# A two-layer transformer forward on one core: each sample's expert routing moved into the attention loop of the next sample

## The reference

```python
h = _layernorm(x) * (1 + ca) + sa
x = x + ga * path_attention(h)          # layer 0, attention: 16 heads of 8
#   L = I + tril(w w^T * beta, -1);  A = solve(L, tril(w k^T, -1))
#   S = q k^T - (q w^T) (beta * A);  P = softmax(S * scale + G_i - G_j, causal);  o = P v
h = _layernorm(x) * (1 + cb) + sb
# layer 0, feed-forward: 16 experts, each token goes to 4
logits = -sum((h - keys) ** 2) + h @ rw.T + rb
topv, topi = top_k(logits, 4);  w = softmax(topv)
x = x + gb * sum(w * (gelu(h @ w1[topi] + b1) @ w2[topi] + b2))
```

## Time and profile before

| | us |
|---|---|
| median of 3 runs (range) | 2480.23 (2475.24 to 2481.59) |
| profiled execution | 2472.11 |
| its span | 2470.3 |
| PE busy | 2084.1 (84%) |
| DVE busy | 1657.9 (67%) |
| POOL busy | 888.7 (36%) |
| ACT busy | 868.9 (35%) |

### The profile page before, as it was taken

The page is one execution under the profiler, slowest core; times in us unless marked ns, Lnnn a source line. Parts: engine busy times, 40 slices in busy tenths (PEclk is TensorE's granted clock), DMA queues, the critical chain, the costliest instruction groups (busy, mean ns, idle before and its releaser), DMA issues. The chain is left out here.

```text
span 2470.3 us, 44381 instructions
## 1 busy us (share of the span) xinstructions
PE 2084.1 (84%) x16530; PEld 1398.4 (57%) x16530; DVE 1657.9 (67%) x3582; ACT 868.9 (35%) x1690; POOL 888.7 (36%) x904
## 2 busy tenths in 40 slices
PE   3888988988988998988988879778799995787885
PEld 2564564654654654644645656545799994344443
DVE  5969579579478488488487444422466665699986
ACT  2031331331331241331332221221165652777782
POOL 1514314225125225125125143632366655433321
PEclk7998988988988988988989887666899997898997
DMA  3105005014023031050050010100622222100000
GB/s 102 35 4 85 2 11 78 2 26 63 2 39 50 3 61 27 3 79 9 3 87 1 16 32 16 34 25 19 219 71 73 72 71 78 49 18 26 5 9 13
DMA packets 133721, 99.85 MB, mean 40 GB/s; under 512 B 13265, under 2 KB 124434, under 8 KB 133394
## 3 DMA queue, kind: packets, MB, share of 16 engines
q1 hardware_dynamic: 124818, 79.05, 16.0%
q0 software_dynamic: 8704, 17.97, 2.2%
HBM read 36.60 MB, written 56.25 MB: 38 GB/s over the span
## 5 line engine op out<-in xcount | busy, mean ns | idle before, releaser
L605 ACT ACTIVATE a_prep<-ps 128x1536 f32<-128x1536 f32 (+1 forms) x112 | 155.7, 1390 | 403.0 <-PE ps L1218 269.6
L832 DVE TENSOR_REDUCE a_mpart<-ps 128x4 f32<-128x512 f32 x320 | 198.7, 682 | 73.4 <-PE ps L1159 46.8
L1761 ACT ACTIVATE b_hid<-ps,b_stage 128x128 f32<-128x128 f32 x576 | 164.0, 368 | 143.2 <-PE ps L1856 130.5
L412 POOL TENSOR_TENSOR a_K<-a_K,a_yU 128x480 f32<-128x480 f32 (+14 forms) x120 | 83.7, 698 | 359.3 <-DVE a_yU L781 358.4
L1746 POOL DMA_INDIRECT rows_y<-b_orow,b_target x144 | 167.0, 1160 | 118.6 <-DVE b_orow L1833 115.2
L418 POOL TENSOR_TENSOR a_X<-a_X,a_flow 128x480 f32<-128x480 f32 (+14 forms) x240 | 181.5, 772 | 77.4 <-DVE a_flow L786 76.4
L1037 PE MATMUL ps<-a_flow,cst 128*128 128x480 f32 (+14 forms) x480 | 180.3, 481 | 6.9 <-DVE a_flow L768 6.1
L1444 POOL DMA_INDIRECT rows_h<-a_flow,r_slot x112 | 108.9, 972 | 177.8 <-DVE a_flow L1612 123.0
L1865 PE MATMUL ps<-b_stage,b_hid 128*128 128x128 f32 x1152 | 153.2, 276 | 1.3 <-ACT b_hid L1761 1.3
L1856 PE MATMUL ps<-b_hTp,b_stage 128*128 128x128 f32 x1152 | 153.9, 277 | 0.0
L1865 PEld LDWEIGHTS ps<-b_stage,b_hid 128*128 128x128 f32 x1152 | 141.0, 193 | 1.7 <-ACT b_hid L1761 1.7
(11 more groups left out here) (466 smaller groups left out, 4641.3 us busy)
## 6 DMA issues: line engine op xcount, KB each, us to landing
rows_h<-a_blank SPq DMA_DIRECT2D x66, 520.0 KB, 12.9
b_hrow<-rows_h SPq DMA_DIRECT2D x144, 65.0 KB
b_w<-in_wexp SPq DMA_DIRECT2D x16, 514.0 KB
c_got<-rows_y SPq DMA_DIRECT2D x32, 256.0 KB, 4.0
rows_y<-b_orow,b_target POOLq DMA_INDIRECT x144
out<-xs SPq DMA_DIRECT2D x8, 256.0 KB, 2.3
cst<-in_const SPq DMA_DIRECT2D x1, 1865.5 KB, 14.7
rows_h<-a_flow,r_slot POOLq DMA_INDIRECT x112
```

Of the source, the lines that this page charges most:

```text
L605: nc.scalar.activation(Pt[:, at:at + width, :], ps[:, 4:4 + width, :], ACT.Exp).then_inc(e_exp.sem, width)
L832: nc.vector.tensor_reduce(mpart[:, i, j, 4 * g:4 * g + 4], ps[:, 4 + n % 4, :].rearrange("p (r j) -> p r j", r=4), AX.X, ALU.max).then_inc ...
L1761: last = nc.scalar.activation(hid[:, p % 2, f, :], ps[:, p % 2, 128 * f:128 * f + 128], ACT.Gelu, bias=stage[:, p % 3, AT_B1 + f:AT_B1 + f ...
```

## The change

The routing of sample b - 1 now runs inside iteration b of the attention loop.

- Iteration 0 is taken out of the loop and has orders of its own for PE and DVE (`ORDER_BEGIN`), with the few steps that begin the routing (`route_begin_vector`, `route_begin_tensor`). The loop is `Fori(1, B - 1)`, six iterations, with `ORDER_ROUTE`, in which r stands beside b and f: 6 letters on PE, 27 on DVE, 8 on ACT and 16 on POOL (its 16 scatters). Taken without r, b and f have the sequence of before.
- In the end stage only sample 6 is routed; its scatters wait one by one for row maxima (`pace`). Sample 7 is routed in the experts, as before.
- The routing's buffers now lie in `mats`, which is free between the 7 chunk steps of the back and the building of the next matrices; `htok` takes its tail. So the norm of the routing waits for the back's chunk steps (`rolled`), the new matrices wait for the routing's end (`V.into`), and those in the tail, 5 of 14, for the landing of the sample's scatters (`R.sent`). Its constants (table 204 KB, b2 8 KB, a gate row 64 KB) are loaded again in each iteration, last in SP's queue.
- The routing's matmuls write PSUM banks 0 to 2, which the front's recurrence uses. So each group of them waits for a step of the recurrence (`gaps`), and six matmuls of the recurrence wait for a routing step (`held`). DVE copies the counts out of PSUM first, and adds into `xs` in 4 pieces.
- `hrows` isn't zeroed in full any more. A region has 640 rows more (EDGE), and after the last slot of sample 6 is given, SP writes 640 rows behind each expert's last row, at an offset read from `R.edge`, and the spare rows: 20 DMAs in the end stage, `R.filled` in the place of `R.zeroed`. `dest` is loaded once, in the first front.

```diff
+ORDER_ROUTE = {
+    'pe': ('bbbbbbbbbfbbbbfbfbfbbbfffbbbbbbbbbbfbbbbbfffbbbbbbbbffbbbfbbbfbbbbfffbbbbbbffbbbbbffbbbbbrbbbbbfbbbb'
...
+    'po': ('bbbbbbbfffffffffffffffbfffbfbbbfbbfrbbrfffrfrffrfffrrfffrfffrrfffrffrffrffrfffrr'),
+}
 ORDER_END = {
...
-    'po': ('bbbbbbbrrrrrrrrrrrrrrrrrrrrrrrrrrrrrrrrrrrrrrrrrrbrrrrrrrrrbbrbbbrbbrbrrrrrrrrrrrrrrrrrrrrrrrrrrrrrr'
-           'rrrrrrrrrrrrrrrrrrrrrrrrrrrrr'),
+    'po': ('bbbbrbbbrrrrrrrrrrbrrrrbrbrbbbbbb'),
 }
...
+        TAIL = 14 * T - NT * TOPK * ROW
+        before_tail = pieces(mats[:, 0:TAIL])
+        table, b2, gate = before_tail(ROUTE["rb"].stop), before_tail(D), before_tail(D)
+        blank = txy[:, 0:EDGE // 128 * ROW]
+        R.place(before_tail(ROUTE_FLAT), table, b2[0:E, :], gate, pieces(mats[:, TAIL:])(NT, TOPK, ROW))
...
-            with sp.Fori(0, B - 1) as b:
-                sp.sem_inc(go.sem, 1)
-                sp.dma_start(gate_row[:, :], dram["s_gate0"][:, bass.ds(b, 1), :]).then_inc(e_gate.sem, 16)
+            gates(0)
+            front()
+            constants(0)
+            close()
+            with sp.Fori(1, B - 1) as b:
+                gates(bass.ds(b, 1))
                 front()
-                for n in range(SHARE):
-                    sp.dma_start(whole[bass.ds(b * SHARE + n, 1)].rearrange("n p f d -> p (n f) d"), blank[:, :].unsqueeze(1).broadcast_to([128, 8, ROW]))\
-                        .then_inc(R.zeroed.sem, 16)
+                constants(bass.ds(b - 1, 1))
                 close()
...
+            gates(B - 1)
+            constants(B - 2)
+            sp.wait_ge(*e_blank())
+            sp.wait_ge(*e_edge())
+            for e in range(E):
+                at = sp.value_load(R.edge[0:1, e:e + 1], min_val=0, max_val=E * CAP - EDGE)
+                sp.dma_start(hrows[bass.ds(at, EDGE), :].rearrange("(p f) d -> p (f d)", p=128), blank).then_inc(R.filled.sem, 16)
...
+            both(2, ORDER)
+            with po.Fori(1, B - 1) as b:
+                both(b + 2, ORDER_ROUTE, b, r=route_pool(nc, po, R, V, hrows))
...
-            weave(ORDER_END['po'], b=back(), r=each(lambda b: route_pool(nc, po, R, hrows, b), B - 1))
+            weave(ORDER_END['po'], b=back(), r=itertools.chain(blanks(), route_pool(nc, po, R, V, hrows, pace=[e_max(8 + 2 * n) for n in range(16)])))
...
                     if over_back and j == 0:
                         ve.wait_ge(*e_kx())
+                    if over_back and j == 0:
+                        ve.wait_ge(*(V.begun() if routing is None else V.into()))
+                    if routing is not None and T * (j + 1) > TAIL:
+                        ve.wait_ge(*R.sent(routing))
...
+                held = {("U", 4): V.hT(), ("X", 5, 0): V.htok(0), ("X", 6, 1): V.logc(), ("U", 7): V.counted(),
+                        ("X", 8, 0): V.turned(), ("X", 9, 1): V.part()} if routing else {("U", 4): V.begun()}
...
+            gaps = {"xT": e_yU(2), "back": e_yX(6), "log": e_yX(9), "count": e_yU(5), "turn": e_yX(12), "bias": e_yX(15)}
+            both(2, ORDER_BEGIN, False, itertools.chain(wait_for(pe, gaps["xT"]), route_begin_tensor(nc, pe, ps, R, V)))
+            with pe.Fori(1, B - 1) as b:
+                both(b + 2, ORDER_ROUTE, True, route_tensor(nc, pe, ps, cst, R, V, gaps))
...
-CAP = B * T
+EDGE = T + PAGE
+CAP = B * T + EDGE
```

More of the change, by code:

```diff
@@ L454, in _, with both @@
             po.sem_inc(over.sem, 1)
-            with po.Fori(0, B - 1) as b:
-                po.wait_ge(go.sem, b + 2)
+            def both(go_at, order, sample=None, **routing):
+                po.wait_ge(go.sem, go_at)
                 po.sem_inc(started.sem, 1)
-                weave(ORDER['po'], b=back(), f=front(True))
+                weave(order['po'], b=back(), f=front(True), **routing)
                 po.wait_ge(*e_uU())
@@ L963, in _, with front @@
             mm = nc.tensor.matmul
-            def front(over_back):
+            def front(over_back, routing=False):
                 pe.wait_ge(*e_xn())
@@ L1278, in _, with both @@
             pe.sem_inc(over.sem, 1)
-            with pe.Fori(0, B - 1) as b:
-                pe.wait_ge(go.sem, b + 2)
+            def both(go_at, order, routing, r):
+                pe.wait_ge(go.sem, go_at)
                 pe.sem_inc(started.sem, 1)
-                weave(ORDER['pe'], b=back(), f=front(True))
+                weave(order['pe'], b=back(), f=front(True, routing), r=r)
                 pe.wait_ge(*e_m())
@@ L1384, in __init__ @@
-        self.e_dest, self.e_share4, self.e_turn, self.e_turned, self.e_bias = ev("dest"), ev("share4"), ev("turn"), ev("turned"), ev("bias")
-        self.e_part, self.e_in = ev("part"), ev("in")
-        self.e_sent = ev("sent", 16 * NT * TOPK)
-    def place(self, table, b2, gate, xn, hT, hsq, part, htok, small, wide, turned):
-        self.table, self.b2, self.gate = table, b2, gate
-        self.xn, self.hT, self.hsq, self.part, self.htok, self.turned = xn, hT, hsq, part, htok, turned
-        take, at = pieces(small), pieces(wide)
+        self.edge = sb("edge", [1, E], I32)
@@ L1484, in route_vector @@
-def route_vector(nc, ve, xs, ps, R, b):
+    act.wait_ge(*V.htok(0))
+    nc.scalar.copy(R.htok[:, :, 1:TOPK, 0:D], R.htok[:, :, 0:1, 0:D].broadcast_to([128, NT, TOPK - 1, D])).then_inc(V.htok.sem, 1)
+    yield
+    act.wait_ge(*V.shift())
+    nc.scalar.activation(R.raw, R.shifted, ACT.Exp).then_inc(V.exp.sem, 1)
+    yield
+    act.wait_ge(*V.turn())
+    nc.scalar.copy(R.turned, ps[0:E, 1, :]).then_inc(V.turned.sem, 1)
+def route_vector(nc, ve, xs, ps, R, V, tile, free=()):
     def line(ap):
@@ L1628, in route_tensor, with gap @@
+    yield
+    ve.wait_ge(*V.part())
+    ve.wait_ge(*V.xn())
+    for t in range(NT):
+        xb = xs[:, tile(t), :]
+        last = nc.vector.tensor_tensor(xb, xb, R.part[:, t:t + 1, :], ALU.add)
+    last.then_inc(V.into.sem, 1)
+def route_tensor(nc, pe, ps, cst, R, V, gaps=None):
     mm = nc.tensor.matmul
     ident = cst[:, CONST["ident"][0]:CONST["ident"][1]]
-    pe.wait_ge(*R.e_xn(b))
-    if b == B - 1:
-        pe.wait_ge(*R.loaded(1))
-    if b:
-        pe.wait_ge(*R.e_hT(b - 1))
+    def gap(name):
+        if gaps:
+            pe.wait_ge(*gaps[name])
+    pe.wait_ge(*V.xn())
+    gap("xT")
@@ L1740, in _ @@
         def _(po):
[L1741 removed]
+            for _ in route_pool(nc, po, R, V, hrows, filled=True):
                 pass
```

555 lines of the change are left out of this document (284 added, 271 removed).

## The result

| | before | after |
|---|---|---|
| median of 4 runs (range), us | 2477.73 (2472.88 to 2481.59) | 2447.10 (2435.78 to 2464.25) |
| ratio (95% interval) | | 0.9881 (0.9846 to 0.9916) |
| profiled execution / span, us | 2472.11 / 2470.3 | 2449.33 / 2447.5 |

The kernel became 1.2% faster, 31 us by the medians, where 100 were forecast; 2447 lies outside the range (2322 to 2440). The direction was right. The runs after spread over 28 us, those before over 9, and the profiled execution after, 2449, lies near their middle.

A forecast was written before the change was run, and what follows sets the result against it. PE was seen as busiest in the loop (161 of 179 us), seven samples' routing as stretching the end stage. End stage -174, loop +78, iteration 0 +1, experts -5 gave -100: 2372, carried to 2378 us; range 2322 to 2440.

The forecast's parts named there:

- The loop: Six attention iterations, each now holding one sample's routing: +13 us an iteration, +78 in all.
- the scatters' term: POOL in the loop: 16 scatters, 20 us, mostly covered by its stalls waiting for DVE; +1 us an iteration.
- The other two terms: Routing's cost in the loop on DVE, +10 us an iteration, and on PE, +2.
- rival 2: Each loop scatter costs the front a share of itself, 8 us an iteration: +48, 2426 us; chance 12%.
- The first leg: In the loop DVE and POOL shut each other out at the shared port: 8 us an iteration.
- The second leg: PE's instructions wait for issue beside scatters: 0.8 us a scatter, 8 us an iteration.
- Rival 4: Loop scatters lie in the front's chain in full, delaying updates, DVE and PE: 33 us an iteration, 2498 us; chance 7%.
- The end stage: Stage after the loop, keeping one sample's routing of seven: from 331 to 157 us, -174.
- the maxima: 40 row maxima of the end stage: 27 us of DVE plus 10.5 of routing, 38 us.
- The other four parts: End stage: start to first maximum 36 us, last maximum to first exp 19, exps 48, last exp to end 16.
- Instruction fetch: Code grows, but queue traffic in the iterations and PEld's wait at the loop's start stay as before: 0.
- The experts: Experts stage: DVE no longer waits 6.02 us for r_dest, -5 us.

The follow-up runs named there:

- e3: Changed kernel without the scatters of samples 0 to 5, only its loop to be read: exps of iterations 2 to 6 52.8 to 54.5 us, six iterations 1155.4 us.
- e8: Changed kernel with two memsets in place of each loop scatter, only its loop to be read: exps of iterations 2 to 6 55.2 to 60.2 us.
- e7: Changed kernel with all 16 scatters of a sample in one burst in the loop, ahead of the updates: ratio 1.0195 against the kernel before.
- e11: Changed kernel with loop written out, scatters later in the exps and no end-stage fillers: 2394.0 us, ratio 0.9916 against the kernel before on its chip.
- e12: Changed kernel with scatters later in the exps and no end-stage fillers, loop kept: 2397.0 us, ratio 0.9924 against the kernel before on its chip.
- e1: Changed kernel with the 20 fills of hrows waiting for the end stage's last row maximum: 2446.2 us, ratio 0.9835 against the kernel before.
- groups 1 and 2: Two sets of four edited versions of the changed kernel, each set on one chip; the kernel before has medians of 2484.8 and 2480.5 us there.
- e5: Changed kernel without the 175 filler matmul steps in TensorE's end stage: 2438.4 us, ratio 0.9739 against the kernel before.

## Why the prediction was wrong

The forecast was -100 and the profiles give -22.8. The 77 us between them are 46 of the loop, 23 of the end stage, 8 of what follows it, less 1 of the first stages.

**The loop (+78, measured +124.3): the step that failed is the scatters' term, +1 an iteration, on the ground that POOL's stalls cover them.** The exps grew by 5.5 to 7.9 us in five iterations and by 19.6 in one, 8.5 on the mean. Without scatters (e3) it is 1.9, with memsets in their place (e8) 4.7, both on other chips' profiles; and the loop without scatters costs +81.7, near the 72 of the forecast without that term. The stall total of the earlier trace rows was no cover: DVE does wait for POOL (19.2 us once with the burst of e7; in the exps of iteration 2 by 2.5 us with the scatters spaced, 0.5 without), PE then waits for DVE, and the clock in the exps is lower than in the kernel before in every iteration, down to 0.74 in one, which is 12.5 us. The other two terms were right: DVE's 10 us stand where they were put (gaps +10.3 an iteration, maxima +1.7).

How the rivals fared here: a term of this size was in rival 2 (8 us an iteration, 2426 in all), and with the end stage as measured its price gives 2449. That is luck, since neither of its mechanisms is there at that size. The first leg, the port, is refuted by DVE's unchanged time. The Trainium skill ("SBUF — State Buffer", "SBUF: two separate sides"), which the prediction cites for it, ties the lock to VectorE operations in a 2-port mode, or with two inputs in SBUF and then only against a GpSimd operation that reads SBUF, and it ties the held-up descriptors to a 2-port operation; the prediction left these conditions out. Which of them the front's steps meet was not tested. The second leg, TensorE's waits for issue, is 0.6 us in the exps. Its price of 0.8 us a scatter came from five stretches, 65 us, picked where PE was emptiest; over all eight runs of scatters it is (133 - 85) / 106 = 0.45. Rival 4's chain is there with a few us, not with 20.

**The end stage (-174, measured -150.7): the step that failed is the maxima, 38 forecast and 64.3 measured.** I took 40 x 0.68 us of DVE plus 10.5 of routing. DVE's 33.7 us are what came. But the bound there is PE: all 175 filler steps stayed in its order while the stage lost half of its length, and 31.5 us of them stand in the maxima. I had seen them in the first paragraph and priced them nowhere. Taking them out does not give 38 either, for without them PE runs at half clock (57.6 us). The other four parts were forecast at 119 and measured at 115.4, but by errors of -7, +5, +3 and -5 that happen to cancel.

**Instruction fetch (0, measured about 6).** "As before" was read off PE alone. DVE's longer body waits 3.5 us at the branch; written out, some 1 us an iteration comes back by the edges, and by the medians of e11 and e12 3 us in all, which is within the noise. That the wait is a fetch is likely by q14's packets, but not shown.

**The experts (-5, measured 0).** A wait was removed; the waits for PE's logits and for the landing of the first page took its place. What follows the end stage is 3.4 us longer in all, and where the rest of that stands was not looked for.

**Right:** the fills are hidden (e1), the zeroing in the loop had cost nothing that shows (maxima 42 to 45 before, 44 to 46 after, with the routing's part in them), the burst of rival 4 exists and the spacing avoids most of it (e7), iteration 0 (+2.6 against +1).

**Open.** Why a burst of scatters holds TensorE up on one chip and not on another, why at the same clock the exps with scatters take 57.4 us on one chip and 56 on another, and what sets off the stretches at half clock in the exps: on the chips of groups 1 and 2, with scatters, up to 37.5 us of an iteration's exps are at half clock, without them up to 17 us, and no run controlled it.

## What to carry to other kernels

When work leaves a stage, recount everything that was tuned to its old length, fillers first: they cost nothing that could be measured in the long stage, and are 31.5 of the 64.6 us of the maxima in the short one. But time them both ways: taken out, their time came back as a lower clock. A row of stalls on the engine that gets the work is not cover for it until each piece is laid beside a stall; ask instead who waits behind the piece. And a gain that rests on a starved engine should be timed on a second chip: the same change gave 0.9881 on one and 0.9951 on another.

## What was not expected of the hardware

- In the same eight bursts of scatters at a pitch of 1.26 us, PE is busy for 85 of 133 us in one profile and for 114 of 133 on another chip, by the same code, and waits for issue for 35 us and 0.2; POOL's own durations are the same (0.96 us).
- The same 14 groups of scores with the same matmuls took 59.3 us at a mean clock of 0.94 and 71.8 at 0.74 in two iterations of one execution.
- 175 filler steps and no fillers give the same end stage on one chip (e7 180.3, e5 180.7 us): the half clock and the fillers' time cancel. On another the fillers cost 5 us (183.5 and 178.4).
